# One gated-delta attention layer between two expert layers: the products of k with k and with q in one matmul of 256 columns over two banks, and a block piece moved ahead of the additions

## The reference, cut to what matters

```python
q, k, v, z = split(hidden @ W_qkvz); b, a = split(hidden @ W_ba)
q, k, v = silu(causal_conv4(q, k, v))          # per channel, 4 taps
q, k = l2norm(q) * 128**-0.5, l2norm(k)
g = -exp(A_log) * softplus(a + dt_bias); beta = sigmoid(b)
def step(state, (qt, kt, vt, gt, bt)):         # one token
    state = state * exp(gt)
    delta = (vt - kt @ state) * bt
    state = state + outer(kt, delta)
    return state, qt @ state
out = rmsnorm(core) * norm_weight * silu(z) @ W_out
```

## Time and profile before

| what | us |
|---|---|
| three runs | 2902.64, 2900.11, 2900.11 (median 2900.11) |
| the profiled execution | 2902.21, of which 2900.5 are the span from the first to the last instruction |
| TensorE busy in the span | 2657.3 (92%) |
| VectorE busy | 1884.2 (65%) |
| ScalarE busy | 1360.2 (47%) |
| TensorE busy from 800 to 1000 us | 198.84 of 200 |
| VectorE busy from 800 to 1000 us | 184.34 of 200 |

### The profile page before, as it was taken

How to read it: one execution, slowest core, us unless ns; L and a number is a source line. 1 busy time by engine, 2 the same in 40 slices (tenths; PEclk the granted TensorE clock), 3 DMA queues, 4 the chain that set the end, 5 groups by cost and what they waited for, 6 DMA issues and landing times. The chain is left out here.

```text
span 2900.5 us, 62348 instructions
## 1 busy us (share of the span) xinstructions
PE 2657.3 (92%) x21920; PEld 2195.9 (76%) x21921; DVE 1884.2 (65%) x3550; ACT 1360.2 (47%) x4371; POOL 694.5 (24%) x967
## 2 busy tenths in 40 slices
PE   5999994556999999999999999999999997699997
PEld 4999994334777777777777777777777776699997
DVE  4111114598999999999999999999987544311111
ACT  1111111434766676676666666666665553011111
POOL 1222221321222322222232231322321111122221
PEclk9999996878999999999999999999999998699999
DMA  7777762345654554555545545546553323677774
GB/s 228 236 218 226 223 186 57 130 134 170 186 175 155 167 170 155 176 162 159 187 144 169 175 145 188 157 155 184 152 166 102 103 65 108 206 224 214 227 219 136
DMA packets 412290, 488.67 MB, mean 168 GB/s; under 512 B 215488, under 2 KB 295872, under 8 KB 412032
## 3 DMA queue, kind: packets, MB, share of 16 engines
q1 hardware_dynamic: 397056, 464.86, 49.6%
q0 software_dynamic: 14976, 20.46, 4.8%
HBM read 348.64 MB, written 138.67 MB: 168 GB/s over the span
## 5 line engine op out<-in xcount | busy, mean ns | idle before, releaser
L530 PE MATMUL f_ps_up<-f_xgT,f_w_up 128*128 128x128 f32 x4368 | 506.4, 277 | 2.0 <-DMA f_w_up<-in_L_ffn_w_dram 2.0
L530 PEld LDWEIGHTS f_ps_up<-f_xgT,f_w_up 128*128 128x128 f32 x4368 | 499.7, 194 | 2.9 <-ACT f_xgT L568 2.8
L597 DVE TENSOR_TENSOR f_hT<-f_hT,f_ps_up 128x512 f32<-128x512 f32 (+1 forms) x156 | 96.9, 621 | 500.7 <-ACT f_hT L576 500.7
L1203 PE MATMUL at_bank<-xnT,at_w_qk 128*128 128x512 f32 x512 | 272.4, 661 | 60.2 <-DVE at_qk L1527 56.7
L1527 DVE SCALAR_TENSOR_TENSOR at_qk<-at_bank,at_taps_qk,at_qk 128x510 f32<-128x510 f32 (+2 forms) x384 | 281.9, 744 | 68.1 <-ACT at_qk L1401 58.9
L1527 DVE SCALAR_TENSOR_TENSOR at_vT<-at_bank,at_taps_v,at_vT 128x510 f32<-128x510 f32 (+2 forms) x384 | 280.4, 744 | 36.8 <-ACT at_vT L1408 27.7
L1793 POOL TENSOR_SCALAR at_small<-at_small 128x4 f32<-128x4 f32 x64 | 17.7, 277 | 1145.1 <-ACT at_squares L1435 1145.1
L576 ACT ACTIVATE f_hT<-f_ps_up 128x512 f32<-128x512 f32 (+1 forms) x156 | 84.9, 544 | 434.5 <-PE f_ps_up L530 434.5
L494 POOL DMA_INDIRECT sums<-f_y,f_row_of x78 | 123.8, 1587 | 540.4 <-DVE f_y L603 540.4
L541 PE MATMUL f_ps_y<-f_w_down,f_hT 128*128 x1092 | 248.8, 379 | 3.8 <-DVE f_hT L597 3.8
L1228 PE MATMUL at_bank<-at_w_vz,xnT 128*128 128x256 f32 x1024 | 243.5, 381 | 7.0 <-DVE at_vT L1527 6.9
(11 more groups left out here) (221 smaller groups left out, 5513.3 us busy)
## 6 DMA issues: line engine op xcount, KB each, us to landing
f_w_up<-in_L_ffn_w_dram SPq DMA_DIRECT2D x156, 896.0 KB, 6.4
at_steps_e<-steps_kept SPq DMA_DIRECT2D x64, 512.0 KB, 6.9
pt_kept<-at_pt_made SPq DMA_DIRECT2D x64, 512.0 KB, 2.7
mt_kept<-at_mt_made SPq DMA_DIRECT2D x64, 512.0 KB, 4.1
at_mt<-mt_kept SPq DMA_DIRECT2D x64, 512.0 KB, 4.0
at_pt<-pt_kept SPq DMA_DIRECT2D x64, 512.0 KB, 4.6
qk_kept<-at_qk SPq DMA_DIRECT2D x64, 256.0 KB, 2.7
ks_kept<-at_ks_made SPq DMA_DIRECT2D x64, 256.0 KB, 2.7
```

The lines of the kernel that those rows point to most:

```text
L530: last = te.matmul(ps_up[hf][w][:, at:at + P], w_up[b][:, w, k, P * j:P * j + P], xgT[b][:, k, :], start=(k == 0), stop=(k == KD - 1))
L597: v.tensor_tensor(part, part, ps_up[hf][1][:, 0:P * (high - low)], ALU.mult).then_inc(h_ready, 1)
L1203: last = te.matmul(proj_bank[ct][:], w_qk[u[0] % 2][:, k, ct * P:(ct + 1) * P], xnT[:, k, UT * u[1]:UT * u[1] + UT], start=(k == 0), stop= ...
```

## The change

1. One matmul makes k·q and k·k of a chunk: k is the loaded operand as before, and q and k of the chunk pass as one moving operand of 2 x 128 columns. Its 256 result columns lie side by side. The results of the four chunks fill two adjoining banks, which are now one tensor, `pair`; its first half stands in for `gen[2]`, its second for `gen[0]`. Step `products` 0 makes chunks 0 and 1 in the first half, step 1 chunks 2 and 3 in the second. One semaphore, `kk_kq_done`, counts both.
2. Each mix now reads both banks (every other 128 columns) and waits for both product steps. So both guards, `bank0_read` and `bank2_read`, wait for both mixes.
3. In `DVE_ORDER` the third piece of `blocks` stands ahead of add 0, and not behind add 1.
4. In `FILL_PE_ORDER` the two transposing steps (`turn`) come before the products.

```diff
 FILL_PE_ORDER = (...
-                 ("project", 1), ("z", 0), ("on_state", 1), ("products", 0), ("y_turn", 0), ("turn", 1), ("inv_n",),
+                 ("project", 1), ("z", 0), ("on_state", 1), ("turn", 1), ("y_turn", 0), ("turn", 0), ("products", 0), ("products", 1), ("inv_n",),
...
-DVE_ORDER = (("inv_x", 32), ("blocks", 0), ("blocks", 1), ("conv_qk", 0), ("conv_qk", 1), ("inv_x", 64), ("add", 0),
-             ("from_state",), ("add", 1), ("blocks", 2), ("blocks", 3), ("conv_v", 2), ("conv_v", 3), ("scan",),
+DVE_ORDER = (("inv_x", 32), ("blocks", 0), ("blocks", 1), ("conv_qk", 0), ("conv_qk", 1), ("inv_x", 64), ("blocks", 2),
+             ("add", 0), ("from_state",), ("add", 1), ("blocks", 3), ("conv_v", 2), ("conv_v", 3), ("scan",),
...
-        bank = [r.ps(f"bank{k}", [P, 512]) for k in range(8)]
-        proj_bank, inv_bank, gen = bank[0:2], bank[2:4], bank[4:8]
+        bank = [r.ps(f"bank{k}", [P, 512]) for k in range(6)]
+        pair = r.ps("pair", [P, 2 * 512])
+        proj_bank, inv_bank = bank[0:2], bank[2:4]
+        gen = [pair[:, 512:1024], bank[4], pair[:, 0:512], bank[5]]
...
 def bank0_read(u, me):
...
+    at_least(pe, s["mt_ready"], seen(u, me, ("products", 1)))
     at_least(pe, s["pt_ready"], seen(u, me, ("products", 1)))
...
 def bank2_read(u, me):
     at_least(pe, s["mt_ready"], seen(u, me, ("products", 0)))
+    at_least(pe, s["pt_ready"], seen(u, me, ("products", 0)))
...
-def products(u, of):
-    me = ("products", of)
+def products(u, half):
+    me = ("products", half)
     pe.wait_ge(s["qk_ready"], 2 * idx(u) + 2)
-    (bank0_read if of else bank2_read)(u, me)
-    q, k = qk[two(u)][:, 0, :], qk[two(u)][:, 1, :]
-    for t in range(Q4):
+    (bank0_read if half else bank2_read)(u, me)
+    for t in (2 * half, 2 * half + 1):
         tt = slice(P * t, P * t + P)
-        last = te.matmul(gen[0 if of else 2][:, tt], k[:, tt], q[:, tt] if of else k[:, tt], start=True, stop=True)
-    last.then_inc(s["kq_done" if of else "kk_done"], 1)
+        last = te.matmul(pair[:, 256 * t:256 * t + 256], qk[two(u)][:, 1, tt], qk[two(u)][:, :, tt], start=True, stop=True)
+    last.then_inc(s["kk_kq_done"], 1)
...
 def mix(u, of):
     dve.wait_ge(s["decay_ready"], idx(u) + 1)
-    dve.wait_ge(s["kq_done" if of else "kk_done"], idx(u) + 1)
+    dve.wait_ge(s["kk_kq_done"], 2 * idx(u) + 2)
     at_least(dve, s["spilled"][1 - two(u)], SPILL * of_two(shift(u, -1)))
-    both = gen[0 if of else 2][:].rearrange("p (t m) -> p t m", m=P).unsqueeze(2).to_broadcast([P, Q4, HV, P])
+    kq_kk = pair[:].rearrange("p (t a m) -> p t a m", a=2, m=P)
+    both = kq_kk[:, :, 0 if of else 1, :].unsqueeze(2).to_broadcast([P, Q4, HV, P])
```

More of the change, by code:

```diff
@@ L862 @@
 FILL_PE_ORDER = (("proj_qk", 0), ("proj_qk", 1), ("state",), ("project", 0), ("on_state", 0), ("proj_v", 2),
-                 ("project", 1), ("z", 0), ("on_state", 1), ("products", 0), ("y_turn", 0), ("turn", 1), ("inv_n",),
+                 ("project", 1), ("z", 0), ("on_state", 1), ("turn", 1), ("y_turn", 0), ("turn", 0), ("products", 0), ("products", 1), ("inv_n",),
                  ("inv_x", 32), ("solve", 0), ("y_turn", 1), ("proj_v", 3), ("turns", 0), ("inv_last",),
-                 ("output", 0), ("turn", 0), ("inv_x", 64), ("solve", 1), ("z", 1), ("products", 1), ("output", 1),
+                 ("output", 0), ("inv_x", 64), ("solve", 1), ("z", 1), ("output", 1),
                  ("turns", 1))
@@ L998, in build_attention @@
                  "ss_done", "scales_step", "vscale_ready", "b_ready",
-                 "kscale_ready", "diag_ready", "decay_ready", "kk_done", "kq_done", "mt_ready",
+                 "kscale_ready", "diag_ready", "decay_ready", "kk_kq_done", "mt_ready",
                  "pt_ready", "v_turned", "qk_turned", "v_ready", "k_ready", "block_step", "low_ready",
@@ L1397, in conv_qk @@
                     act.wait_ge(s["qk_projected"], 2 * idx(u) + ct + 1)
-                    at_least(act, s["kq_done"], idx(u) - 1)
+                    at_least(act, s["kk_kq_done"], 2 * (idx(u) - 1))
                     at_least(act, s["spilled"][two(u)], SPILL * (of_two(u) - 1))
```

## The result

The changed kernel takes 2918.39 us (median of 4 runs, 2916.99 to 2919.44) where the kernel before took 2901.38 in the same measurement: a ratio of 1.0057, 95% interval 1.0042 to 1.0072. It is slower by 17 us. The forecast was 2903.0, no change, with a range that ended at 2910.

What follows compares the result with a forecast made beforehand. TensorE was taken to bound steady rounds, with output 1 newly waiting for mix 1. Steady rounds +2.8, fill -0.9, first output rounds +1.0 gave +2.9 us: 2903.0 from a median of 2900.11, range 2896 to 2910.

Steps and rivals of the forecast that it cites:

- The wait that comes with it: Output 1 on TensorE must wait for mix 1, starting at S + 11.96 in every steady round, idling 0.68 us.
- S: Time origin of a round: the start of its first proj_v matmul on TensorE; times are us after it.
- I take 0.20: Way from mix 1's end on VectorE to output 1's start on TensorE: 0.20 us, bounded by 0.15 and 0.21.
- From output 1 to the next S: TensorE's time from output 1's start to the next round's first proj_v matmul, claimed as 15.93 us.
- rival 2: VectorE's way through the round is longer than assumed: 2907.9 us at +0.10 a round, 2912.8 at +0.2; chance 0.22.
- The fused products: TensorE's two product steps: 1.73 us instead of 2.00, saving 0.27 a unit, without effect because output 1 waits.
- the comparison with z: TensorE's z step, 8 records of 256 columns in 1.73 us, taken as the time of the fused product steps.
- 34 ns more: TensorE matmul records: two of 128 columns (125 ns each) claimed to cost 34 ns more than one of 256 (216).
- The block piece: VectorE's piece moved ahead of add 0: convolution at S + 2.64 every round; the round into part 1 27.99 us.
- the cover: VectorE's idle time ahead of add 0, 1.32 us in a part 0 round, where the moved piece now stands.
- Rival 1: TensorE stays the only bound and keeps the saving of 0.27 us a unit: 2882.8 us; chance 0.08.
- Rival 4: TensorE's clock falls because of its new 0.68 us idle each round, adding some 137 us; chance 0.01.

## Why the prediction was wrong

- **The wait that comes with it: right, its size too small.** Output 1 waits for mix 1 in every round. Mix 1 ends at S + 11.76 and the convolution begins at S + 2.64, as written, except that both are up to 0.07 later in rounds of part 1 (in the row above 1235.80 - 1233.09 = 2.71). The step that failed is "I take 0.20" for the way from mix 1 to output 1: it measured 0.36 (0.38 on the mean of 48 rounds). Of the two rows that bounded it one (0.15) has, in the trace's records, no further wait instruction between the released one and the weight load, the other (0.21) has one; output 1 has two, and a third behind its first weight load. Rows with shorter lists are no upper end for a longer one. The list of the changed kernel, shown with the change, held the answer: what stands behind the wait that ends last is worked off only after it, at 0.105 us a piece in this trace.
- **From output 1 to the next S: 15.93 forecast, 16.00 measured.** After an idle the group of eight takes 1.13 instead of 1.06: its first matmul's record lasts 0.35 instead of 0.28, and the second starts 0.185 behind it instead of 0.112. The wait instruction between the first two weight loads isn't the cause, for these start 0.109 apart all the same, and the first group of the earlier trace rows, which has none there, shows the same: 0.46 for two records, where 0.11 + 0.28 make 0.39. So the prediction's own rows held this term. Together these two terms make 28.12 of 27.89 (28.11 in most rounds); the mean round is 28.16, mostly from the longer ways in 10 rounds and the up to 0.07 in part 1 rounds. Forecast for the mean was 27.92: 0.24 x 48 = 11.6 us are missing here, of 15 between 2903.0 and 2918.4; about one more lies in the last rounds, 1.3 in the kernel before, whose median was 2901.38 this time and not 2900.11, and the rest is within the scatter. The prediction had named this sign: output waits and rounds are longer than 28, so a term of the loop was too small.
- **This was rival 2**: "a way of 0.30 after mix 1", with 2912.8 for 0.2 more a round, and a chance of 0.22. The range ended at 2910, below its own upper price.
- **The fused products: 1.73 forecast, 1.93 measured, and without effect, as forecast.** The step that failed is the comparison with z: the 2.00 of before held a wait of 0.2 for ScalarE's copy, which the fused form doesn't remove. "0.125 each" was the 2.00 spread over 16 records; they come every 0.112. That the products' time does no harm shows in output 1's idle of 0.5 behind them in every round; the run that put the second step behind z gained nothing either (2916.56), though only 0.04 of its 0.2 reached output 0.
The Trainium skill, page "TensorE: Matmul & The Clock Gate", section "Back-to-back issue gap", was set aside in the prediction for "34 ns more". The records give 2 x 111.6 - 216 = 7 ns more for two short matmuls than for a long one, nearer to the page's 2.5 ns than to the 34.
- **The block piece: right on the convolution, wrong on its price.** "In the other rounds VectorE is there earlier than TensorE" holds in the changed kernel only because output 1's wait is longer than VectorE's limit (28.11 against 27.92), and the 27.99 for the round into part 1 measured 28.09 there. Taken alone the move gains and loses the same (ratio 1.0). The step that failed here is the cover: the earlier trace rows's 1.32 us of idle time ahead of add 0 is that of part 0; in part 2 it was 0.85, add 0 could start 1.1 later, and the piece takes 2.28.
- **Rival 1 (2882.8)** was not had in any fused form that was run: its saving of 0.27 a unit was 0.06 and a wait. **Rival 4** didn't come: TensorE was idle for 0.5 us in every round and the clock stayed at 1.00.
The Trainium skill, same page, section "A second HAM failure mode: psum-queue depth-cycling", tells of a kernel whose clock swung with short idles between groups of matmuls; this trace doesn't agree, at 1.00 in every window from 800 to 2000 us.

What isn't settled: why the way was 0.39 to 0.53 in 10 rounds (in each the extra lies between the first and the second wait instruction, 0.14 to 0.28 instead of 0.105), why the first matmul after an idle has the longer record, and how the last 2 to 3 us divide between the drain and scatter.

## What to carry to other kernels

Sharing a buffer between two results makes its next writer wait for both readers: before counting what the fusion saves, find the later reader's end and the next writer's start, and count what is queued behind. A wait that is new costs its place in the list too; where the last to come is known, ask for it so that it is checked last (in this kernel, first in the code). Work moved ahead of a wait is free only up to the time to spare there, so a long piece is better cut in two, one for each gap: that alone makes this kernel 0.5% faster (2885.66 us), and 0.64% with the second products behind z (2881.68 us), without any fusion.

## What the runs showed of the hardware

- A wait instruction of TensorE that stands behind the last released one costs about 0.105 us, and a matmul whose last wait is the released one starts 0.05 to 0.06 us after the end of VectorE's record; with the released wait in an instruction of its own and two more behind it, it was 0.36.
- f32 matmul records of 128 columns came every 0.112 us and of 256 columns every 0.216 at full clock; a moving operand of two pieces of 128 columns passes at the same 0.216. The first record of 128 columns behind an idle lasted 0.35 instead of 0.28.
- VectorE's multiplication of 128x1024 from PSUM took 1.22 us from one bank and from every other 128 columns of two adjoining banks alike; cut into 128x512, an instruction took 0.68 to 0.69, and two of them 0.06 more than one whole.
